# Cross-attention: the product with the values in f32 on two tiles of 64 rows

## What is computed

```python
queries = _rope((LN(x) @ Wq.T) ...)          # [16, 32, 64, 128]
keys = _rope((ctx @ Wk.T) ...)               # [16, 8, 128, 128], repeated for 4 query heads
values = (ctx @ Wv.T) ...                    # the same, without rope
scores = where(causal, queries @ keys.T * 128 ** -0.5, min)   # 64 queries x keys
ctx = softmax(scores) @ values
x = x + ctx.reshape(...) @ Wd.T
```

## Time and profile before

| | |
|---|---|
| median of 3 runs | 805.54 us (805.36 to 805.68) |
| profiled execution, first to last instruction | 802.9 us |
| PE busy | 780.4 us, 4112 matmul records |
| PE weight loads | 643.9 us |
| DVE busy | 511.5 us, 927 instructions |
| ScalarE busy | 390.6 us, 692 instructions |
| POOL busy | 467.9 us |
| mean granted clock | 0.985 of full speed |

### The profile page before, as it was taken

One profiled execution on the slowest core, in us unless ns is written; L12 is line 12 of the kernel. 1 busy time (PEld: TensorE's weight loads), 2 busy tenths in 40 slices (PEclk: granted clock), 3 DMA queues, 4 the chain that ended last, 5 costly groups with the idle time before them and its releaser, 6 DMA issues.

```text
span 802.9 us, 11770 instructions
## 1 busy us (share of the span) xinstructions
PE 780.4 (97%) x4112; PEld 643.9 (80%) x4112; DVE 511.5 (64%) x927; ACT 390.6 (49%) x692; POOL 467.9 (58%) x363
## 2 busy tenths in 40 slices
PE   6899999999999999999999999999799999999998
PEld 4688888888888888888888888888688777777786
DVE  6866465655655565565555566466857777779855
ACT  3546436453543735455373454537254666564220
POOL 4538546764754675485376458637543687865350
PEclk9889999999999999999999999999799999999999
DMA  8102101200210120030012003001101110001002
GB/s 296 53 2 78 53 1 52 78 0 0 78 52 0 52 78 0 0 97 34 0 52 78 0 3 124 3 0 41 40 1 52 40 51 2 2 19 63 14 1 105
DMA packets 11338, 34.09 MB, mean 42 GB/s; under 512 B 1456, under 2 KB 1584, under 8 KB 11312
## 3 DMA queue, kind: packets, MB, share of 16 engines
q1 hardware_dynamic: 11312, 33.75, 12.8%
HBM read 31.65 MB, written 2.10 MB: 42 GB/s over the span
## 4 chain that ended last, share of the span: by engine, by line
PE 90%; DVE 6%; issue 2%; ACT 1%; POOL 1%; DMA 1%; SPq 0%; ACTq 0%; POOLq 0%
PE pj L1110 53%; PE pj L1261 8%; PE sc L1141 7%; PE sc L1306 3%; PE pv L1330 2%; PE tp L1319 2%; PE pv L1156 2%; PE pv L1157 2%; PE tp L1149 2%; DVE sm L755 1%; PE pj L1402 1%; PE pj L1465 1%; PE tp L1134 1%; DVE al L857 1%; PE pv L1465 1%
## 5 line engine op out<-in xcount | busy, mean ns | idle before, releaser
L398 POOL TENSOR_TENSOR sw<-sw,cst 128x512 f32<-128x512 f32 x79 | 109.4, 1385 | 62.5 <-ACT sw L539 62.3
L410 POOL TENSOR_TENSOR sm<-sm,mx 128x512 f32<-128x512 f32 x64 | 67.3, 1052 | 133.9 <-DVE mx L790 133.9
L563 ACT ACTIVATE sm<-sm 128x512 f32<-128x512 f32 x64 | 40.5, 633 | 149.5 <-POOL sm L410 149.1
L538 ACT ACTIVATE sw<-pj 64x512 f32<-64x512 f32 x80 | 47.7, 596 | 127.0 <-DVE t L780 126.7
L1110 PE MATMUL pj<-xh,wqh 128*128 128x512 f32 x252 | 103.3, 410 | 0.0
L1110 PE MATMUL pj<-wdh,ch 128*128 128x512 f32 x256 | 101.8, 398 | 0.2 <-issue 0.2
L415 POOL TENSOR_TENSOR sm<-sm,rz 128x512 f32<-128x512 f32 x64 | 66.9, 1045 | 58.4 <-DVE rz L797 58.4
L1110 PE MATMUL pj<-wdh,cl 128*128 128x512 f32 x256 | 99.8, 390 | 0.0
L1110 PE MATMUL pj<-wdl,ch 128*128 128x512 f32 x256 | 99.7, 389 | 0.0
L1110 PE MATMUL pj<-xh,wql 128*128 128x512 f32 x252 | 99.6, 395 | 0.0
L1110 PE MATMUL pj<-xl,wqh 128*128 128x512 f32 x252 | 99.3, 394 | 0.0
(11 more groups left out here) (201 smaller groups left out, 1759.0 us busy)
## 6 DMA issues: line engine op xcount, KB each, us to landing
raw<-in_w_x SPq DMA_DIRECT2D x40, 512.0 KB, 4.0
qr<-in_ctxT SPq DMA_DIRECT2D x4, 512.0 KB, 7.1
X<-in_x SPq DMA_DIRECT2D x4, 512.0 KB, 7.5
raw<-in_w_s SPq DMA_DIRECT2D x4, 512.0 KB, 3.6
out<-X SPq DMA_DIRECT2D x8, 256.0 KB, 2.1
raw<-in_w_s SPq DMA_DIRECT2D x4, 256.0 KB, 3.1
raw<-in_w_o SPq DMA_DIRECT2D x2, 512.0 KB, 3.7
raw<-in_w_b SPq DMA_DIRECT2D x2, 512.0 KB, 6.2
```

The lines of the kernel that those rows point to most:

```text
L398: pool.tensor_tensor(sw[par][:, :].rearrange("p (b s) -> p b s", s=S), sw[par][:, :].rearrange("p (b s) -> p b s", s=S), rep(cst[:, C_SIN: ...
L410: pool.tensor_tensor(s3, s3, per_group(mx[:, c, :], 8), ALU.subtract).then_inc(subbed, 1)
L538: act.activation(sw[par][0:64, :], src[64:128, :], ACT.Copy)
```

## The change

`pv_x` now takes the probabilities and the values in plain f32 as they come from the transposes, without hi and lo parts. The transposes of two batches stand one over the other: the even batch has its 64 keys in rows 0 to 63, the odd one in rows 64 to 127. A call is four matmuls over 64 rows, 256 columns each, in turn on the upper and the lower 64 rows, into one bank for even and one for odd batches. For this `scores_x` writes its blocks in another order. ScalarE copies the operands whole (`v_copy`, `p_copy`, one instruction each, semaphore `tp_c`); `v_lo` and `p_lo` and their places on DVE are gone. `ch` and `cl` have a new layout, so that `c_hi` and `c_lo` are one instruction over 1024 columns instead of four over 256, and `out_x` reads them by it. Gaps keep all other tiles at their addresses. The tile that is zeroed for the warm-up matmuls is another one. `v_copy` and `p_copy` stand where `v_hi` and `p_hi` stood in ScalarE's stream, and every wait for `tp_lo` is one for `tp_c`.

```diff
-        v2h, v2l = [None, None], [None, None]
+        vv = [None, None]
         for i in range(2):
-            v2h[i] = sb(xs, f"v2h{i}", [P, HB, DH], F32R)
-            v2l[i] = sb(xs, f"v2l{i}", [P, HB, DH], F32R)
-        ch = sb(xs, "ch", [P, REP, HALF], F32R)
-        cl = sb(xs, "cl", [P, REP, HALF], F32R)
-        pt = [sb(xs, f"pt{i}", [P, 1024], F32R) for i in range(2)]
+            vv[i] = sb(xs, f"vv{i}", [P, HB // 2, DH])
+            sb(xs, f"gap_v{i}", [P, 1536])
+        ch = sb(xs, "ch", [P, XCH, 8, P], F32R)
+        cl = sb(xs, "cl", [P, XCH, 8, P], F32R)
+        pt = [None, None]
+        for i in range(2):
+            pt[i] = sb(xs, f"pt{i}", [P, 512])
+            sb(xs, f"gap_p{i}", [P, 512])
...
+        pv4 = pv[:, :, :].rearrange("p a (n q) -> p a n q", q=S)
+
+        def by_bank(t, c):
+
+            return t[:, c, :, :].rearrange("p n (a q) -> p a n q", q=S)
...
-            pool.memset(pt[0][:, 0:640].bitcast(F32), 0.0).then_inc(warm_set, 1)
+            pool.memset(ch[:, 0, 0:5, :].bitcast(F32), 0.0).then_inc(warm_set, 1)
...
-            def v_hi(u, h):
+            def v_copy(u, h):
                 act.wait_ge(tp_t, 3 * u + 1)
-                for odd in range(2):
-                    for half in range(2):
-                        last = act.activation(
-                            v2h[h][64 * half:64 * half + 64].rearrange("p (b o) d -> p b o d", o=2)[:, :, odd, :],
-                            tp[64 * odd:64 * odd + 64, 0, :].rearrange("p (b d) -> p b d", d=DH), ACT.Copy)
-                last.then_inc(tp_hi, 1)
-
-            def p_hi(u, c):
+                act.activation(vv[h][:, :, :].rearrange("p b d -> p (b d)"), tp[:, 0, :], ACT.Copy).then_inc(tp_c, 1)
+
+            def p_copy(u, c):
                 act.wait_ge(tp_t, 3 * u + 2 + c)
-                for hp in range(2):
-                    last = act.activation(pt[c][0:64, :].rearrange("p (b r q) -> p b r q", b=4, r=2)[:, :, hp, :],
-                                          tp[64 * hp:64 * hp + 64, c, :].rearrange("p (b q) -> p b q", b=4), ACT.Copy)
-                last.then_inc(tp_hi, 1)
+                act.activation(pt[c][:, :], tp[:, c, :], ACT.Copy).then_inc(tp_c, 1)
...
             def c_hi(u, c):
                 act.wait_ge(pv_t, 2 * u + c + 1)
-                for r in range(REP):
-                    last = act.activation(
-                        ch[:, r, c * 256:(c + 1) * 256].rearrange("p (b q) -> p b q", q=S),
-                        pv[:, :, :].rearrange("p a (b r q) -> p (a b) r q", b=2, r=REP)[:, :, r, :], ACT.Copy)
-                last.then_inc(pv_hi, 1)
+                act.activation(by_bank(ch, c), pv4, ACT.Copy).then_inc(pv_hi, 1)
...
-            def v_lo(u, h):
-                dve.wait_ge(tp_hi, 3 * u + 1)
-                for odd in range(2):
-                    for half in range(2):
-                        r = slice(64 * half, 64 * half + 64)
-                        last = dve.tensor_tensor(
-                            v2l[h][r].rearrange("p (b o) d -> p b o d", o=2)[:, :, odd, :],
-                            tp[64 * odd:64 * odd + 64, 0, :].rearrange("p (b d) -> p b d", d=DH),
-                            v2h[h][r].rearrange("p (b o) d -> p b o d", o=2)[:, :, odd, :].bitcast(F32), ALU.subtract)
-                last.then_inc(tp_lo, 1)
-
-            def p_lo(u, c):
-
-                dve.wait_ge(tp_hi, 3 * u + 2 + c)
-                for hp in range(2):
-                    p4 = pt[c][:, :].rearrange("p (b r q) -> p b r q", b=4, r=2)[:, :, hp, :]
-                    last = dve.tensor_tensor(p4[64:128], tp[64 * hp:64 * hp + 64, c, :].rearrange("p (b q) -> p b q", b=4),
-                                             p4[0:64].bitcast(F32), ALU.subtract)
-                last.then_inc(tp_lo, 1)
-
             def c_lo(u, c):
                 dve.wait_ge(pv_hi, 2 * u + c + 1)
-                for r in range(REP):
-                    cs = slice(c * 256, (c + 1) * 256)
-                    last = dve.tensor_tensor(
-                        cl[:, r, cs].rearrange("p (b q) -> p b q", q=S),
-                        pv[:, :, :].rearrange("p a (b r q) -> p (a b) r q", b=2, r=REP)[:, :, r, :],
-                        ch[:, r, cs].bitcast(F32).rearrange("p (b q) -> p b q", q=S), ALU.subtract)
-                last.then_inc(pv_lo, 1)
+                dve.tensor_tensor(by_bank(cl, c), pv4, by_bank(ch, c).bitcast(F32),
+                                  ALU.subtract).then_inc(pv_lo, 1)
...
                 sum_rec(2 * u + 1, 1)
-                p_lo(u, 0)
                 rope_cos(u + 1, 1 - h, 1, False)
-                p_lo(u, 1)
                 rope_cos(u + 1, 1 - h, 2, False)
                 if h == 0:
...
                     out_add(u, h, 1)
-                    v_lo(u + 1, 1 - h)
                     out_add(u, h, 2)
...
                             mask_max(2 * u + 2, 0)
-                            v_lo(u + 1, 1 - h)
...
-                        last = pe.matmul(sc[:, c, (2 * b + hp) * S:(2 * b + hp + 1) * S],
+                        blk = (b // 2 * 2 + hp) * 2 + b % 2
+                        last = pe.matmul(sc[:, c, blk * S:(blk + 1) * S],
                                          qr[h][:, bb, 2 * hp:2 * hp + 2, :], kr[h][:, bb, :],
                                          start=True, stop=True)
                 last.then_inc(scored, 1)
...
             def pv_x(u, h, c):
-                for b in range(4):
-                    o = pv[:, b // 2, (b % 2) * 256:(b % 2 + 1) * 256]
-                    p = pt[c][:, b * 256:(b + 1) * 256]
-                    pe.matmul(o, v2h[h][:, 4 * c + b, :], p, start=True, stop=False)
-                    last = pe.matmul(o, v2l[h][:, 4 * c + b, :], p, start=False, stop=True)
+                for bp in range(2):
+                    for bo in range(2):
+                        rows, cols = slice(64 * bo, 64 * bo + 64), slice(bp * 256, (bp + 1) * 256)
+                        last = pe.matmul(pv[:, bo, cols], vv[h][rows, 2 * c + bp, :], pt[c][rows, cols],
+                                         start=True, stop=True)
                 last.then_inc(pv_t, 1)
 
             def out_x(u, i, bank=0):
-                tok = slice(i * P, (i + 1) * P)
-                three(pj[:, (i + bank) % 2, :], [((ch[:, r, tok], cl[:, r, tok]), (wdh[:, r, :], wdl[:, r, :]))
-                                        for r in range(REP)]).then_inc(outp, 1)
+                c, at = i // 2, i % 2 * REP
+                three(pj[:, (i + bank) % 2, :],
+                      [((ch[:, c, at + r, :], cl[:, c, at + r, :]),
+                        (wdh[:, r, :], wdl[:, r, :])) for r in range(REP)]).then_inc(outp, 1)
...
-                pe.matmul(pv[:, 0, :], pt[0][:, 0:P], pt[0][:, P:640], start=True, stop=True)
+                pe.matmul(pv[:, 0, :], ch[:, 0, 0, :], ch[:, 0, 1:5, :], start=True, stop=True)
...
-                    pe.wait_ge(tp_lo, 3 * u + 1)
+                    pe.wait_ge(tp_c, 3 * u + 1)
```

More of the change, by code:

```diff
@@ L194, in build @@
         tp_t = sem("tp_t")
-        tp_hi = sem("tp_hi")
-        tp_lo = sem("tp_lo")
+        tp_c = sem("tp_c")
         scored = sem("scored")
@@ L590, in _ @@
             ln_hi_tile(7)
-            v_hi(0, 0)
+            v_copy(0, 0)
             def phase(u, h, g, nxt):
@@ L597, in phase @@
                 copy_v(u + 1)
-                p_hi(u, 0)
+                p_copy(u, 0)
                 swap_halves(u + 1, 1 - h, 1, False)
-                p_hi(u, 1)
+                p_copy(u, 1)
                 if h == 0:
@@ L611, in phase @@
                 c_hi(u, 1)
-                v_hi(u + 1, 1 - h)
+                v_copy(u + 1, 1 - h)
                 if h == 0 and nxt == "loop":
@@ L892, in _ @@
             ln_lo(7)
-            v_lo(0, 0)
             def phase(u, h, g, nxt):
@@ L1216, in phase @@
                     pe.wait_ge(normed, 2 * u + c + 1)
-                    pe.wait_ge(tp_lo, 3 * u + 1)
+                    pe.wait_ge(tp_c, 3 * u + 1)
                     p_transposes(u, c)
                     project(2 + c)
-                pe.wait_ge(tp_lo, 3 * u + 2)
+                pe.wait_ge(tp_c, 3 * u + 2)
                 pv_x(u, h, 0)
                 project(4)
-                pe.wait_ge(tp_lo, 3 * u + 3)
+                pe.wait_ge(tp_c, 3 * u + 3)
                 v_transposes(n, 1 - h)
```

## The result

The changed kernel takes 810.34 us (median of 9 runs, 807.64 to 812.21), the kernel before 805.56 us (9 runs): a ratio of 1.0049, with an interval of 1.0035 to 1.0062. It is slower, by 4.8 us.

What follows compares the result with a forecast made beforehand. The prediction took PE, busy 97%, as the bound: a span of 802.9 + 9.9 (calls) - 3.6 (waits) - 1.3 (behind the loop) = 807.9 us, plus 2.6 around it, gave 810.5 us; range for 8 in 10: 797.5 to 820.

Steps and rivals of the forecast that it cites:

- Two tiles run side by side in four slots: In `pv_x`, matmuls on the even and odd 64-row tiles overlap, so a call's matmuls take 0.86 us.
- staggered: Rival: records in `pv_x` start in program order, five slots, 1.08 us before the size change; 817.6 us in all, chance 0.12.
- no overlap: Rival: row tiles in `pv_x` run one after the other, 1.73 us before the size change; 838.4 us in all, chance 0.11.
- The change of size costs 0.41 us: Around each `pv_x` call, going into the small tiles and out again costs PE 0.41 us.
- the allowance of 2 x 0.05 for the larger loads: At each `pv_x` call, weight loads of 128 columns instead of 64 add twice 0.05 us to 0.31.
- +0.31 us a call: Each of the 32 `pv_x` calls takes 1.27 us against 0.96, together +9.9 us.
- The wait of 0.24 us a unit goes: In the loop, PE no longer waits for ScalarE's swap (L539): 15 units x 0.24 = -3.6 us.
- A unit +0.38 us: Each unit of the loop gets longer by 2 x 0.31 - 0.24 = 0.38 us.
- Behind the loop -1.3 us: Without `v_lo` on the chain, about 1.0 us, and with an earlier second `pv_x` of the last unit, about 0.3.
- The span: The profiled execution of the whole kernel, 802.9 us before, was forecast at 807.9 us after.

Runs made afterwards that it cites:

- e6: The changed kernel with all four matmuls of a `pv_x` call on the upper 64 rows, leaving out the odd batches: 840.18 us, ratio 1.0423.
- e3: The changed kernel with the two `pv_x` calls of a unit back to back, in the 14 units of the loop: 806.05 us, ratio 1.0002.
- e1: The changed kernel with the four matmuls of `pv_x` reordered, both of the even tile, then both of the odd one: 811.60 us, ratio 1.0081.
- e4: The changed kernel with the same four f32 matmuls over all 128 rows instead of 64, even and odd batches summed: 825.88 us, ratio 1.0262.
- e9: The changed kernel with PE's eight fp32r matmuls a call over 128 rows again, fed by ScalarE's single copies, without lo parts: 801.91 us, ratio 0.9960.
- e2: The kernel before with the new layout of `ch` and `cl` alone, so `c_hi` and `c_lo` are one instruction each: 801.44 us, ratio 0.9959.
- e5: e2 with `v_hi` and `v_lo` of the last unit moved ahead of `c_hi` and `c_lo` behind the loop: 802.83 us, ratio 0.9961.
- e8: The kernel before with matmuls whose results nobody reads in PE's idle places, the same lines as in e7: 801.71 us, ratio 0.9944.
- e10: The changed kernel with matmuls whose results nobody reads in the same idle places of PE as in e8: 803.94 us, ratio 0.9976.
- e7: e5 with unread matmuls where PE idles, 14 ahead of the first scores and 12 behind the loop: 795.80 us, ratio 0.9876.

## Why the prediction was right

The forecast was 810.5 us and the measured time 810.34, and by its steps:

- *Two tiles run side by side in four slots*: right, and shown: pairs in the narrow views, 0.86 us less than on one tile (e6), 0.86 us for the second call of e3. It was inferred from tiles of 64 columns; those of 64 rows behave the same. The rivals "staggered" and "no overlap" are out. That the order in the program could matter, on which the staggered rival rested and my theory for e1 too, was wrong (e1).
- *The change of size costs 0.41 us*: right. After, a call with what is late behind it is 1.24 us, 0.38 over its slots; e3, which saves one going in and out a unit, gives back 0.44. With 0.31, without the allowance of 2 x 0.05 for the larger loads, the sum would have come out too low; that the loads are the reason wasn't tested. That it is the size and not the type is shown by e4, and that it isn't the use of two tiles by e6.
- The Trainium skill, "TensorEngine Tiling (Array Packing)", Key Properties, has the tiling mode's change drain TensorE, and tiles that work in parallel; for tiles of 64 rows both halves agree with the runs, with 0.4 us a time and e6's 1.92 against 1.06 us.
- *+0.31 us a call*: 0.30 by e9 (0.60 a unit).
- *The wait of 0.24 us a unit goes*: right, 0.25 by e9. But I tied it to `p_lo` mostly, and merging `c_hi` and `c_lo` does it by itself (e2); `p_lo` alone wasn't tried.
- *A unit +0.38 us*: 0.35 to 0.36.
- *Behind the loop -1.3 us*: from the last scores to the end the span of before had 802.9 - 567.5 = 235.4 us and that of after 808.5 - 574.7 = 233.8, -1.6. The last unit's two calls add 0.6 to it. So the gains are 2.2 us, more than forecast: 1.06 in front of the addition, 0.3 in front of the second `pv_x`, 0.55 from the clock (4.47 us for the 12 records instead of 5.02, which I had left open by 2 us either way), and 0.4 at a later place, where PE had waited before its third chunk of self-attention scores.
- *Not in the sum*: the head. The profile after has its first scores 0.8 us later and its first unit 1.2 us longer than the rest of the difference explains (39.55 - 37.99 = 1.56, of which 0.36 is the unit's). The clock from 40 to 54 us, before and after:

```profile
40.00:54.00 14.00, 12.43 (x56) 11.03 (x57) 9.74 (x15) 4.87 (x9) 3.33 (x4) 0.76 0.00 1
...
40.00:54.00 14.00, 11.62 (x48) 10.69 (x49) 7.40 (x11) 2.28 (x5) 4.14 (x4) 0.63 0.00 1
```

0.76 and 0.63: in slices of 1 us it stands at 0.50 from 43.6 to 50 us before and from 41.5 to 51.6 after. The prediction left the clock of the head out of its sum without a word. e2 and e5, with the same code there, differ in the same way, so it need not come from the change; that was not settled by a run. The span was forecast at 807.9 and is 808.5 us. The 0.6 is these 2.0 us of head, less 0.9 behind the loop (-1.6 instead of -1.3 + 0.6), less 0.5 in the units, which grew by 0.36 instead of 0.38 and the last one of the loop's kind by 0.16 only. The agreement of the medians to 0.2 us is in part luck: 2.0 us that no term stood for were made up by 1.4 us by which the units and the stretch behind the loop came out lower, and the runs of the changed kernel spread over 4.6 us, with mean clocks from 0.989 (807.64 us) to 0.980 (812.21 us).

What stays open: why the clock's lower stretches last longer in one run than in another. e8 had more of them in the head than e10, and no edit here bears on that. And e8 gained 3.8 us by filling where e7 had gained 7. Its mean clock from 748 to 753 us was 0.66, and e10's 0.66, in a place that was not filled, where e7's was 1.00; and its chain behind the loop still goes through `v_lo` and `c_lo`. I didn't take these apart.

## What to carry to other kernels

Where PE is the bound, count slots and changes of the array's tile size, not matmuls: four f32 matmuls on two half tiles took 0.86 us where eight fp32r ones over the whole array take 0.96, but each going in and out of the half tiles cost 0.4 us on top, so such calls should be joined (e3). Relief of an engine that isn't the bound is worth only the waits of PE that hang on it; here merging small instructions gave that by itself (e2), and was faster than the rewrite. Look for idle places of PE that are followed by a stretch at the lower clock: matmuls without use in them gave 7 us in e7, 6.4 in e10 and 3.8 in e8, where the whole change had moved 4.8.

## What the runs showed of the hardware that I had not expected

- Matmuls of two tiles of 64 rows run side by side also when the program has all of one tile's ahead of the other's: the second tile's records started 0.01 us behind the first's in e1, and the time was within 0.01 us a unit.
- A matmul in f32 over 64 rows is as long as one over 128: 8 records take 1.92 us with the pause on one tile (e6) and 1.73 without it over the full rows (e4).
- PE's mean clock from 40 to 54 us was 0.63 or 0.76 of full speed (part of the stretch at 1.2 GHz, the rest at 2.4) in the kernels before and after, e2 and e5, in which PE idled for 3 us ahead of the first scores, and from 0.66 to 0.76 in e1, e3, e4, e6 and e9, which idle there too. It was 1.00 in e7, e8 and e10, in which that time was filled with matmuls, and these had zeros as operands.
